# Graph attention and expert layer: a strip's second half in the step after its attention, its placing one step after that

## What is computed

```python
x = x + gnn(layernorm(x), adj, W, a)     # x: 8192 x 256, adj: 8192 x 8192, some 4 ones in a row
#   Wh = h @ W; e = leaky_relu(Wh@a1 + (Wh@a2).T), masked by adj; elu(softmax(e) @ Wh)
x = x + ffn(layernorm(x))
#   idx = argmax(x @ router_w.T + router_b) over 32 experts
#   relu(relu(x @ W1[idx] + b1[idx]) @ W2[idx] + b2[idx])
```

## Time and profile before

| | us |
|---|---|
| median of 3 runs | 1371.22 |
| lowest and highest | 1370.53, 1373.62 |
| the profiled execution | 1381.51 |
| its span | 1379.9 |
| granted TensorE clock, mean | 0.679 of full |
| DVE busy | 1067.8 (77%) |
| PE busy | 837.0 (61%) |
| ACT busy | 731.7 (53%) |
| POOL busy | 614.0 (44%) |

### The profile page before, as it was taken

How to read it: one execution, slowest core, us unless ns; L and a number is a source line. 1 busy time by engine, 2 the same in 40 slices (tenths; PEclk the granted TensorE clock), 3 DMA queues, 4 the chain that set the end, 5 groups by cost and what they waited for, 6 DMA issues and landing times.

```text
span 1379.9 us, 24246 instructions
## 1 busy us (share of the span) xinstructions
PE 837.0 (61%) x3116; PEld 636.2 (46%) x3116; DVE 1067.8 (77%) x4589; ACT 731.7 (53%) x1359; POOL 614.0 (44%) x651
## 2 busy tenths in 40 slices
PE   3766735656666565666656666566566774177664
PEld 2444424445445454444445445444454653055443
DVE  5878748888888888888888888888888664355553
ACT  3656746556665566655666556665563111055553
POOL 2111135444554445444455445454455772245453
PEclk9888856665555655566555665556655665599997
DMA  7999978887888878888788887888872245544442
GB/s 260 314 330 335 329 292 325 347 316 294 318 331 329 324 295 320 330 328 322 298 322 325 330 317 294 326 327 329 316 294 91 75 99 104 156 121 119 125 127 64
DMA packets 110969, 365.64 MB, mean 265 GB/s; under 512 B 28840, under 2 KB 62081, under 8 KB 78163
## 3 DMA queue, kind: packets, MB, share of 16 engines
q1 hardware_dynamic: 80610, 302.25, 58.5%
q0 software_dynamic: 28288, 61.66, 13.9%
q10 hardware_dynamic: 2034, 1.37, 0.3%
HBM read 352.05 MB, written 32.05 MB: 278 GB/s over the span
## 4 chain that ended last, share of the span: by engine, by line
DVE 37%; issue 30%; PE 14%; DMA 7%; DVEq 4%; ACT 3%; POOL 3%; POOLq 1%; ACTq 0%; SPq 0%
DVE top_word L854 6%; DVE top_pos L860 4%; PE psL L1510 4%; DMA out_x<-yb,tok 3%; DVE diag L1059 3%; PE psW L1431 3%; ACT sg L699 2%; PE psT L1501 2%; PE psL L1511 2%; POOL G_all L590 2%; DVE xn L1103 2%; DMA G_all<-wh_table,idx 1%; DVE el L1076 1%; DVE st L909 1%; DVE yb L1376 1%
## 5 line engine op out<-in xcount | busy, mean ns | idle before, releaser
L590 POOL DMA_INDIRECT G_all<-wh_table,idx x384 | 393.9, 1026 | 248.3 <-issue 121.3
L699 ACT ACTIVATE sg<-raw_all,minus_half 128x2048 fp8e4<-128x2048 int32 x256 | 504.0, 1991 | 0.0
L1491 PE MATMUL psO<-G_all,diag 128*128 128x256 f32 x640 | 280.5, 621 | 95.1 <-issue 76.2
L1491 PEld LDWEIGHTS psO<-G_all,diag 128*128 128x128 f32 x640 | 199.8, 324 | 144.9 <-issue 99.6
L724 ACT ACTIVATE xT<-psT 128x256 f32<-128x256 f32 x64 | 24.5, 383 | 399.2 <-PE psT L1501 320.0
L860 DVE FIND_INDEX8 top_pos<-top_word,sg 128x8 uint32<-128x512 f32 x256 | 175.6, 686 | 1.7 <-issue 0.6
L854 DVE MAX8 top_word<-sg 128x8 f32<-128x512 f32 x256 | 174.8, 683 | 0.4
L612 POOL DMA_INDIRECT regions<-x,posu x64 | 67.8, 1059 | 149.1 <-DVE posu L1141 142.2
L653 POOL DMA_INDIRECT out_x<-yb,tok x81 | 81.9, 1011 | 88.6 <-DVE yb L1376 62.3
L1431 PE MATMUL psW<-w_aug,xT 128*128 128x258 f32 x256 | 85.2, 464 | 8.6 <-ACT xT L691 8.6
L606 POOL TENSOR_TENSOR x<-ve,minus_half 128x1 f32<-128x1 f32 x64 | 36.2, 565 | 106.4 <-DVE x L1099 105.5
(11 more groups left out here) (209 smaller groups left out, 1918.0 us busy)
## 6 DMA issues: line engine op xcount, KB each, us to landing
raw_all<-in_adj SPq DMA_DIRECT2D x256, 1024.0 KB
xb<-regions SPq DMA_DIRECT2D x84, 130.0 KB
wh_table<-G_all POOLq DMA_DIRECT2D x8, 1040.0 KB, 10.5
w_sb<-in_x SPq DMA_DIRECT2D x8, 1024.0 KB, 8.0
xr<-in_x SPq DMA_DIRECT2D x64, 128.0 KB
G_all<-wh_table,idx POOLq DMA_INDIRECT x384
w_sb<-in_L_ffn_W SPq DMA_DIRECT2D x2, 1024.0 KB
w_sb<-in_L_ffn_W SPq DMA_DIRECT2D x4, 512.0 KB
```

The costliest lines, as they stand in the source:

```text
L590: pool.indirect_dma_start(out=G[par][:, k, :], out_offset=None, in_=table[:, :], in_offset=bass.IndirectOffsetOnAxis(ap=idx[par][:, k:k + ...
L699: act.activation(sg[par][q][:, :], raw[q], ACT.Sign, bias=minus_half[:, 0:1], saturate=False).then_inc(a_sg, 1)
L1491: pe.matmul(psO[par][:, 0:D], diag[:, k, :], G[par][:, k, 0:D], start=(k == 0), stop=False)
```

## The change

Post runs on strip u - 1 and place on strip u - 2; the x rows of strip u are loaded in step u. The list ends with step 65, and W1's quarters go to steps 63, 64 and 65. The parities of the buffers follow. The order of the calls inside a step stays.

```diff
         def does(u):
-            return Does(ahead=u + LAG + 1 < NS, search=u + LAG < NS, attend=u < NS, fetch=u + 1 < NS, prepare=u + 2 < NS, load=1 <= u < NS + 1,
-                        post=2 <= u < NS + 2, place=3 <= u < NS + 3)
+            return Does(ahead=u + LAG + 1 < NS, search=u + LAG < NS, attend=u < NS, fetch=u + 1 < NS, prepare=u + 2 < NS, load=0 <= u < NS,
+                        post=1 <= u < NS + 1, place=2 <= u < NS + 2)
...
-            peeled(NS - 2, NS + 3)
+            peeled(NS - 2, NS + 2)
...
-                for part in {NS: (0,), NS + 1: (1,), NS + 2: (2, 3)}.get(u, ()):
+                for part in {NS - 1: (0,), NS: (1,), NS + 1: (2, 3)}.get(u, ()):
...
                 if do.load:
-                    load_x(u - 1, 1 - par)
+                    load_x(u, par)
...
                 if do.post:
-                    inverse_std(u - 2, par)
+                    inverse_std(u - 1, 1 - par)
                 if do.place:
-                    scatter(u - 3, 1 - par)
+                    scatter(u - 2, par)
...
                 if do.post:
-                    attention_sum(u - 2, par)
+                    attention_sum(u - 1, 1 - par)
...
-                t, w, y = u + LAG, u - 2, u - 3
+                t, w, y = u + LAG, u - 1, u - 2
...
                 if do.place:
-                    ranks(u - 3)
+                    ranks(u - 2)
...
                 if do.post:
-                    post_transposes(u - 2)
-                    logits(u - 2)
+                    post_transposes(u - 1)
+                    logits(u - 1)
```

More of the change, by code:

```diff
@@ L754, in step @@
                 if do.post:
-                    elu_exp(u - 2)
+                    elu_exp(u - 1)
                 if do.ahead:
@@ L759, in step @@
                 if do.post:
-                    transposes2(u - 2)
+                    transposes2(u - 1)
                 if do.ahead:
@@ L1208, in step @@
                 if do.post:
-                    post_x1(w, par, half_up(w, par), None if isinstance(w, int) and w < 2 else half_done(w, par))
+                    post_x1(w, 1 - par, half_up(w, 1 - par), None if isinstance(w, int) and w < 2 else half_done(w, 1 - par))
                 if do.search:
@@ L1214, in step @@
                 if do.post:
-                    post_stats(w, par)
+                    post_stats(w, 1 - par)
                 if do.search:
@@ L1218, in step @@
                 if do.post:
-                    post_mean(w, par)
+                    post_mean(w, 1 - par)
                 if do.search:
@@ L1222, in step @@
                 if do.post:
-                    post_variance(w, par, w)
+                    post_variance(w, 1 - par, w)
                 if do.search:
@@ L1234, in step @@
                 if do.place:
-                    place_position(y, 1 - par)
+                    place_position(y, par)
                 if do.search:
@@ L1238, in step @@
                 if do.post:
-                    post_norm(w, par)
+                    post_norm(w, 1 - par)
                 if do.search:
```

## The result

| | before | after |
|---|---|---|
| median | 1372.42 us (4 runs, 1370.53 to 1373.94) | 1359.90 us (4 runs, 1357.81 to 1362.16) |
| ratio | | 0.9917, 95% interval 0.9896 to 0.9938 |
| the profiled execution | 1381.51 | 1360.98 |

What follows compares the result with a forecast made beforehand. The prediction took DVE's pace in the middle stage to bound the kernel. Its terms, -7.94 + 1.10 - 0.9 + 1.5 = -6.2 us, taken from the median 1371.22, gave 1365.0 us, range 1361.5 to 1370.0.

Steps and rivals of the forecast that it cites:

- What bounds the kernel: Middle stage: DVE sets the pace, and post need not wait for the previous step's weighted sum; no new loop wait.
- Term 1: End of the middle stage: one round of post and place goes, so the last stage starts earlier, -7.94 us.
- the rival in which it does not come off: Last stage's start hangs on something that does not move, so no gain from the dropped step: +1.7 us, chance 0.06.
- Term 2: First steps: post and place work starts a step earlier on DVE, partly absorbed by waits, +1.10 us (0 to 2.79).
- Term 3: Loops: one 32 ns PE register instruction gone 28 times on the way to the logits, -0.9 us (-2.0 to +1.1).
- Term 4: Strip 63's gather: W1's quarters issued directly behind W2 and b1 delay the gathered rows, +1.5 us (0 to 4.7).
- the first rival: Strip 63's gather: POOL's queue takes its turns, W1 costs nothing; -7.7 us in all, 1363.5 us, chance 0.22.
- The sign of being wrong that I had named: Loops: the prediction is wrong if a loop step moves by more than 0.05 us.
- a turn of the loops gets longer: Loops: moved DVE register instructions add 0.2 us per step, 11.2 us; +5.9 overall, 1377.1 us, chance 0.05.

Runs made afterwards that it cites:

- the filled kernels: The kernel before, and before_offset, each with 12 unread products of ones after each weighted sum: 1361.94 us (0.9925) and 1357.67 us (0.9893).
- before_again: The kernel before, unchanged, timed and profiled once more: 1372.11 us, ratio 0.9998.
- before_dve_only: The kernel before with semaphore pe_lg started one higher, moving VectorE's register instruction from L1107 to L1075: 1371.75 us, ratio 1.0005.
- before_offset: The kernel before with semaphores a_x2 and pe_lg started one higher; TensorE's L1498 register instruction gone, VectorE's moved: 1365.26 us, ratio 0.9951.
- before_pe_only: The kernel before with only semaphore a_x2 started one higher, removing TensorE's register instruction at L1498: 1366.35 us, ratio 0.9963.
- offset_nops: before_offset with four empty TensorE instructions written in the place of L1498; the trace shows no row for them: 1363.07 us, ratio 0.9933.
- before_swap: The kernel before with TensorE's two waits ahead of the transposes in the other order, register instruction kept: 1369.44 us, ratio 0.9969.
- after_again: The changed kernel, unchanged, timed and profiled once more: 1362.17 us, ratio 0.9926.

## Why the prediction was wrong, point by point

- **What bounds the kernel: right.** DVE sets the pace, its waits for the logits are what can be won in the loop, and post finds the sum of the step before ready: ACT waits for PE at L713 once in the whole run, 1.5 us, in step 1, covered by a wait that shrank from 3.79 to 1.80. DVE waits at L854 for none of it.
- **Term 1, the last step goes, -7.94: right.** From L1030 of strip 63 to the last L1108 it is 26.4 us in the mean of nine profiles of before and its variants (25.6 to 27.0), and 18.6 in the five of the change and its variants with W2 in its old place (17.8 to 19.0): -7.8. From the last L1108 to the end it is 207.5 us in the mean in the nine and 208.0 in the five, so the last stage started earlier by that; the rival in which it does not come off is out.
- **Term 2, the first steps get fuller, +1.10: right, some 0.6 low.** +1.4 in the first pair of profiles, of which 0.47 in step 1, 0.68 in step 2 and 0.24 in step 3, where I had 0, 1.10 and 0. From L1030 of step 1 to that of step 4 the nine profiles give 42.2 us in the mean (41.8 to 42.6) and the five 44.0 (43.7 to 44.7): +1.7.
- **Term 3, register instructions, -0.9 with the lower end at -2.0: this is the step that failed.** The mechanism was right (PE's L1498, on the way to the logits) and VectorE's side rightly at nothing. The size was wrong: removed alone it gave -5.1, with the other -6.7 and -9.2, moved ahead of the wait -4.3, between the filled kernels -4.4; some 6 us in the mean. I priced it by its own duration in the row, 0.032 us. In the way it costs 0.10, which moving the same instruction ahead of the wait gives back: 2.8 us. The other 3 are not shown to come from anywhere. The intervals of -5.1, -4.3 and -4.4 hold 2.8 as well, those of -6.7 (-9.7 to -3.6) and -9.2 don't. A clock that does better when the transposes come earlier would explain it, but the profiles don't show one. From the transposes to L1108 a loop step takes 2.60, 2.52 and 2.51 us in the mean in before, before_again and before_dve_only, 2.49 in before_offset, before_pe_only and offset_nops, 2.52 in before_swap; two executions of one kernel differ by as much or more (2.54 in after, 2.42 in after_again). What is missing is a pair in which the clock is the same on both sides.
- **Term 4, W1 behind W2, +1.5: wrong.** It costs nothing that the trace shows: the wait at strip 63 was 6.77 us against 6.82, where I had 8.3. I took the gather's 24 packets that were left when b1 ends, but W1 stands behind b1 in SP's queue, and the gather is through before W1's first packet. That W2 makes the wait was read rightly (0.56 us with W2 early). It was the first rival, with 0.22. The rule of the Trainium skill (DMA: Bandwidth & Descriptors, Queues, rings and completion order) gave the right sum, 1.5 us less, but the trace does not test it here: W1 and the gather never had packets under way at the same time.
- **Sum.** -7.8 + 1.7 - 6 + 0 = -12.1, measured -12.5 and -10.1. Of the 4 to 6 us missed, term 3 is the larger part and term 4 has 1.5. The sign of being wrong that I had named came: a loop step moved by more than 0.05 us, by 0.12 in the first pair of profiles and 0.15 in the second.
- **The rival "a turn of the loops gets longer"** asked for the wrong sign: I had written that 0.1 us per step decides, and did not ask what 0.1 us less would give. It also rests on a wrong reading. Of the 1.1 us between the loop step (15.69) and step 3 (14.60 from L1030 to L1030), 0.7 is the wait for the logits, which step 3 does not have; it is not about 1 us of register work.

## What to carry over

A register instruction between a wait that is really waited for and the work behind it costs more than its own duration, here 0.10 us (L1498) and 0.05 us (L1507) for 0.032, every time; such instructions belong ahead of the wait, and a shift of a semaphore's start can make two waits share a register. A table of differences in instructions should be read against the line where the slowest engine waits, and both signs of each priced by the gap in the trace, not by the duration in the row. After an edit of a semaphore's start, look at every wait on it, and after writing a delay, look for its rows in the trace. Where the slowest engine waits for short products of TensorE, look at their durations and the granted clock first: products of nothing in its gaps were worth 15 us on the change, more than the change itself.

## What was not expected of the hardware

- The same transposes take 0.41 or 0.66 us, the same logits 0.54 or 0.96, in neighbouring steps of one loop, at a granted clock of 1.0 or 0.5 of full. 18 products of 128x128 per step, 1.3 us of TensorE's time, put all but one of the 50 loop steps on the fast side (granted clock of the loop 0.61 to 0.69), and the kernel gained 1.3% (0.9771 against 0.9900).
- One register instruction of 32 ns on TensorE behind a wait added 0.10 us ahead of the transposes and 0.05 us ahead of the logits, and nothing to be seen ahead of the wait.
- The wait for the last gather is 2.8 to 3.8 us in most executions and 6.8 in others, with the same kernel (before 6.82, before_again 3.51), and the wait for the gather before it is short where this one is long. What chooses is open.
